# Four conditional layers on one core: products of the weights made first and kept in tables, against two dense layers for every tile of tokens

## The chip, the cores and the metric

The kernel runs on one core of a Trainium2 chip. The core has TensorE (matrix products), VectorE, ScalarE and GpSimd (elementwise work), and SyncE, called SP, which here only issues transfers. They run their own instruction streams and meet at semaphores. The metric is the device time of one execution in microseconds; lower is better.

## The reference

x holds 64 batches of 64 tokens of 1024 numbers. Four layers are added to it, one after the other:

```
x = x + x @ W0.T + 2 * sum over experts e of gate[e] * (x @ A0[e].T) @ B0[e].T
x = x + (Wc[cond[batch]].T mixing the 64 tokens of a batch)
x = x + (x @ B2[id2[batch]].T) @ A2[id2[batch]].T
x = x + x @ W3.T + b3 + 2 * (x @ A3[id3[batch]]) @ B3[id3[batch]]
```

The gates of the first layer are a softmax over the two largest of eight logits, x @ Wr.T plus 5 for the language of the batch. Ranks are 16; there are 8 experts, 16 mixing matrices of 64x64, 64 adapters in the third layer and 32 in the fourth. The four layers are linear but for the gates. All is fp32.

## The kernel before

A tile is 128 tokens, two batches, and there are 32. Every fp32 operand of a dense product is split into a rounded part (hi, type fp32r) and the rest (lo), and a product takes three passes: hi by hi, lo by hi, hi by lo. ScalarE makes the hi part by a rounding copy (`round_to`, L380) and VectorE the lo part by a subtraction (`rest`, L497).

At the start the chunks of W0, B0 and W3, 17 of 512 KB, go through four staging buffers: GpSimd adds the identity for the residual (L348), ScalarE rounds, VectorE or GpSimd subtracts. Both dense weights then stay on the chip.

The tiles run in a software pipeline: step i does the front of tile i (layers 1 to 3) and the back of tile i - 1 (layer 4). Python writes the first two and the last two steps out; those between are a hardware loop (`steps`). TensorE's order in a step is: dense pieces of layer 1 (`layer0`, L711; three pieces of 392, 384 and 384 columns, where the first also holds the expert ranks and the logits), the up product of layer 3 of the tile before (`layer2_up`, L769), the transpose of the gated ranks (L838), the expert rows (`layer0_up`, L752), the dense pieces of layer 4 (`layer3`, L734; up to 384, 352 and 352 columns), mixing in fp32 (L872), the transpose of the stacked ranks (L882), the down product of layer 3 (L892), and the up rows of layer 4 (`layer3_up`, L776). The sum of layer 4 is read from PSUM with the bias added (L696) into outb, and stored.

SP's program holds every transfer of a tile, in an order written out by hand. Where a batch chooses a matrix, SP loads its index from ids_sb into a register first (L232) and then issues a transfer from the chosen row (L241):

```python
return sp.value_load(ids_at[0:1, which, t, b:b + 1], min_val=0, max_val=n - 1)
...
chosen = [index(which, t, b, table.shape[0]) for b in range(BT)]
...
for b in range(BT):
    sp.dma_start(into(b), table[chosen[b]]).then_inc(arrived, 16)
```

ScalarE and VectorE too run through a fixed order in each step: what waits there holds up what is behind it.

Of the kernel before, what the change touches and what calls it, by code (L numbers as in the profile page):

```python
# [5 lines left out]
P = 128  # L6
TOKENS = 128
HALF = 512


def at(i, n):

    return isinstance(i, int) and i == n


class Piece:
# [3 lines left out]
    def __init__(self, shared, start, end):  # L20
        self.x = slice(start, end)
        lead = shared if start == 0 else 0
        self.own = slice(lead, lead + end - start)
        self.bank = slice(0, lead + end - start)
        self.w = slice(0 if start == 0 else shared + start, shared + end)


def cut(shared, edges):
    return [Piece(shared, a, b) for a, b in zip(edges, edges[1:])]


def build(nc, x, W0, A0, Wr, B0, Wc, A2, B2, W3, bias3, A3, B3, lang_ids, ids, out):
# [4 lines left out]
    TILES = x.shape[0]  # L37
    KB = W0.shape[1]
    D = W0.shape[2]
    RANK = B2.shape[3]  # L40
    EXPERTS = Wr.shape[2]
    ER = EXPERTS * RANK
    BT = TOKENS // Wc.shape[1]
    TB = Wc.shape[1]
    BR = BT * RANK
    BANDS = P // BR
    HL = ER + EXPERTS
    HALVES = D // HALF
    D3W = 2 * BR

    PIECES0 = cut(HL, (0, 256, 640, D))
    PIECES3 = cut(D3W, (0, 320, 672, D))
    KH = KB // HALVES
    LANG_BIAS, SCALE0, SCALE3 = 5.0, 2.0, 2.0
    STAGES = 4
    CH_W0, CH_B0, CH_W3, CHUNKS = 0, KB, KB + 1, 2 * KB + 1
    COND, AD2, AD3 = range(3)

    ctx = ExitStack()
    with ctx:  # L60
# [5 lines left out]


        X3_HI, X3_LO, UP3, OUTB = range(CHUNKS - STAGES, CHUNKS)
        stage = [None] * STAGES
        with ExitStack() as stage_ctx:  # L70
            for n in (X3_HI, X3_LO, UP3, OUTB):
                stage[n % STAGES] = stage_ctx.enter_context(nc.sbuf_tensor(f"stage{n % STAGES}", [P, D], F32))
        x3 = pair("x3", [P, KB, TOKENS])
        up3 = sb("up3", [P, D], F32R)
        outb = sb("outb", [P, D])

        w0 = pair("w0", [P, KB, HL + D])
        b0 = pair("b0", [P, D])
        w3 = [sb("w3_hi", [P, KB, D3W + D], F32R),
              sb("w3_lo", [P, KB, D], F32R)]  # L80
        d3 = w3[0][:, :, 0:D3W].rearrange("p k (c b r) -> p k c b r", c=2, b=BT)
        bias_row = sb("bias_row", [P, D])
        xraw = sb("xraw", [P, KB, TOKENS])
        xT = pair("xT", [P, KB, TOKENS])
        with nc.sbuf_tensor("x1", [P, D], F32) as x1:
            pass
        x2 = pair("x2", [P, D])
        upraw = sb("upraw", [P, D])
        up2raw, up3raw = upraw[0:BR, :], upraw[BR:2 * BR, :]
        up2 = sb("up2", [P, D], F32R)  # L90
        d2raw = sb("d2raw", [P, BT, KB, RANK])
        d3raw = sb("d3raw", [P, BT, KB, RANK])
        d2 = sb("d2", [P, KB, 2, BT, RANK], F32R)
        mixraw = sb("mixraw", [P, P])
        mix = sb("mix", [P, P])
        wrraw = sb("wrraw", [P, KB, EXPERTS])
        ident = sb("ident", [P, P])
# [3 lines left out]
        own_batch = sb("own_batch", [BR, BT, TB])  # L101
        iota_e = sb("iota_e", [P, EXPERTS])
        rbias = sb("rbias", [P, TILES, EXPERTS])
        hpart = sb("hpart", [P, BR])
        hsum = sb("hsum", [P, BT, RANK])
        hstack = sb("hstack", [P, BANDS, BT, RANK], F32R)
        h2 = sb("h2", [BR, TOKENS])
# [19 lines left out]

        ps_x1 = [bank(f"ps_x1_{n}") for n in range(len(PIECES0))]
        ps_x23 = [bank(f"ps_x23_{h}") for h in range(HALVES)]
        ps_out = [bank(f"ps_out_{n}") for n in range(len(PIECES3))]  # L130
        ps_d3 = ps_out[0]
        ps_h3T, ps_hgT = ps_x1[2], ps_out[1]
        hi, lo = 0, 1

        def ps_hl(t):

            return ps_x23[1] if at(t, 0) else ps_x1[0]

        def ps_h2(t):

            return ps_out[2] if at(t, 0) else ps_x1[1]
# [3 lines left out]

        def sems(name, n=HALVES):
            return [sem(f"{name}{h}") for h in range(n)]


        ld_x, ld_mix, ld_d2, ld_up2, ld_d3, ld_up3 = map(sem, ("ld_x", "ld_mix", "ld_d2", "ld_up2", "ld_d3", "ld_up3"))  # L150
        ld_ids, ld_lang, ld_bias, ld_a0, ld_wr = map(sem, ("ld_ids", "ld_lang", "ld_bias", "ld_a0", "ld_wr"))
        ld_stage = [sem(f"ld_stage{s}") for s in range(STAGES)]
        st_out = sem("st_out")

        pe_hl, pe_xT, pe_hgT, pe_d2, pe_d3, pe_h3T = map(sem, ("pe_hl", "pe_xT", "pe_hgT", "pe_d2", "pe_d3", "pe_h3T"))
        pe_x2, pe_x3 = map(sems, ("pe_x2", "pe_x3"))
        pe_x1, pe_out = sems("pe_x1", len(PIECES0)), sems("pe_out", len(PIECES3))

        act_w, act_w0d, act_x, act_exp, act_d2, act_up2, act_d3, act_up3, act_hgT, act_fold, act_h2T, act_h3T = map(
            sem, ("act_w", "act_w0d", "act_x", "act_exp", "act_d2", "act_up2", "act_d3", "act_up3", "act_hgT", "act_fold", "act_h2T", "act_h3T"))  # L160
        act_x2, act_x3 = map(sems, ("act_x2", "act_x3"))
        act_x1 = sems("act_x1", len(PIECES0))

        dve_w, dve_w0d, dve_x, dve_diff, dve_hg, dve_up2, dve_d3, dve_up3, dve_hgT, dve_d2, dve_own, dve_h2T, dve_h3 = map(
            sem, ("dve_w", "dve_w0d", "dve_x", "dve_diff", "dve_hg", "dve_up2", "dve_d3", "dve_up3", "dve_hgT", "dve_d2", "dve_own", "dve_h2T", "dve_h3"))
        dve_x2, dve_x3 = map(sems, ("dve_x2", "dve_x3"))
        dve_out = sems("dve_out", len(PIECES3))

        pool_const, pool_w, pool_lo, pool_mix = map(sem, ("pool_const", "pool_w", "pool_lo", "pool_mix"))

        dve_lang, dve_fold, dve_hpart, dve_hsum, dve_h3hi = map(sem, ("dve_lang", "dve_fold", "dve_hpart", "dve_hsum", "dve_h3hi"))
        dve_lg, dve_top, dve_topi, dve_topf, dve_gden, dve_grec, dve_gw0, dve_gw1, dve_gsel, dve_gates = map(
            sem, ("dve_lg", "dve_top", "dve_topi", "dve_topf", "dve_gden", "dve_grec", "dve_gw0", "dve_gw1", "dve_gsel", "dve_gates"))


        PLAN = {"x1 0": 2, "up2 0": 2, "h2 0": 1, "gates 1": 1, "hgT 1": 2}
        assert sum(PLAN.values()) == KB


        POOL_LO = (CH_W3, CH_W3 + 2, CH_W3 + 4)  # L180

        def split_done(n):

            own = n in POOL_LO
            return pool_lo if own else dve_w, sum((m in POOL_LO) == own for m in range(n + 1))


        EXP_AFTER = 3

        def planned(stage):  # L190
            first = CH_W3
            for name, n in PLAN.items():
                if name == stage:
                    return range(first, first + n)
                first += n
            return ()

        CONSTS = 8

        def steps(engine, step):  # L200


            for i in (0, 1):
                step(i, True, i > 0, True)
            with engine.Fori(2, TILES - 1) as i:
                step(i, True, True, True)
            step(TILES - 1, True, True, False)
            step(TILES, False, True, False)

        def split_parts(n):  # L210

            if n < CH_B0:
                return w0[lo][:, n, HL:], w0[hi][:, n, HL:]
            if n == CH_B0:
                return b0[lo][:, :], b0[hi][:, :]
            return w3[lo][:, n - CH_W3, :], w3[hi][:, n - CH_W3, D3W:]

        block = ctx.enter_context(nc.Block())


        @block.sync
        def _(sp):
            ids_at = ids_sb[:, :].rearrange("o (w t b) -> o w t b", w=3, b=BT)

            def load_x(t):

                if not at(t, 0):
                    sp.wait_ge(dve_x, t)
                sp.dma_start(xraw[:, :, :], x[t]).then_inc(ld_x, 16)
# [4 lines left out]
            def load_chosen(t, which, table, into, free, arrived):  # L234

                chosen = [index(which, t, b, table.shape[0]) for b in range(BT)]

                if not at(t, 0):
                    sp.wait_ge(free, t)
                for b in range(BT):  # L240
                    sp.dma_start(into(b), table[chosen[b]]).then_inc(arrived, 16)  # L241

            def load_mix(t):
                load_chosen(t, COND, Wc, lambda b: mixraw[b * TB:(b + 1) * TB, b * TB:(b + 1) * TB], pool_mix, ld_mix)

            def load_down(t, which, raw, table, free, arrived):
                load_chosen(t, which, table, lambda b: raw[:, b, :, :], free, arrived)
# [4 lines left out]
            def load_chunk(n):  # L252

                if n >= STAGES:
                    sp.wait_ge(*split_done(n - STAGES))
# [696 lines left out]
```

## Time and profile before

| what | value |
|---|---|
| median of 3 runs | 995.66 us (994.34 to 996.8) |
| the profiled execution | 994.18 us, span 992.2 us |
| TensorE busy | 979.3 us, 99% of the span |
| VectorE, ScalarE, GpSimd busy | 53%, 37%, 4% |
| DMA | 61.58 MB, mean 62 GB/s |
| mean granted TensorE clock | 0.996 |

The span runs from the first to the last instruction that the profiler saw. Busy shares are of the span. Matmuls are pipelined, so that a single one's time overlaps the next one's; what a matmul costs in a stream is the distance between starts.

### The profile page before, as it was taken

How to read it: one execution, taken by the hardware profiler on the slowest of the kernel's cores; microseconds unless marked ns; L12 is line 12 of the kernel's file. 1: busy time of each engine (PE TensorE's matmuls, PEld its weight loads, DVE VectorE, ACT ScalarE, POOL GpSimd, SP SyncE). 2: the span in 40 equal slices, each digit the busy share in tenths (PEclk: the TensorE clock that was granted, in tenths of full speed). 3: DMA queues.
4: the chain of work that ended last, by engine and by line, in shares of the span. 5: the costliest groups of instructions: out<-in, count | busy, mean ns of one | idle time of the engine just before them, and what ended most of it. 6: DMA issues, size and time to landing. Idle time of an engine off the chain costs nothing.

```text
span 992.2 us, 18376 instructions
## 1 busy us (share of the span) xinstructions
PE 979.3 (99%) x6394; PEld 973.6 (98%) x6394; DVE 530.5 (53%) x1236; ACT 370.3 (37%) x660; POOL 38.1 (4%) x63
## 2 busy tenths in 40 slices
PE   8899999999999999999999999999999999999998
PEld 7799999999999999999999999999999999999998
DVE  5875545545455455455465454554564554554544
ACT  4653332433333343323333323433333333243331
POOL 3600000000000000000000000000000000000000
PEclk9999999999999999999999999999999999999999
DMA  7621111111111111111111111111111111111001
GB/s 257 222 86 55 54 51 54 60 60 39 59 44 59 58 44 57 62 44 58 59 44 54 44 59 58 55 48 59 44 58 59 44 54 50 55 58 62 18 33 43
DMA packets 40046, 61.58 MB, mean 62 GB/s; under 512 B 10849, under 2 KB 27362, under 8 KB 40034
## 3 DMA queue, kind: packets, MB, share of 16 engines
q1 hardware_dynamic: 40034, 61.43, 18.6%
q8 instruction: 6, 0.10, 0.0%
q14 instruction: 6, 0.05, 0.0%
HBM read 44.63 MB, written 16.78 MB: 62 GB/s over the span
## 4 chain that ended last, share of the span: by engine, by line
PE 95%; DVE 3%; DMA 1%; ACT 1%; issue 0%; SPq 0%; POOL 0%; DVEq 0%; POOLq 0%
PE ps_x L711 39%; PE ps_out L734 38%; PE ps_x L872 6%; PE ps_x L752 5%; PE ps_x L892 3%; PE ps_x L769 3%; PE ps_out L776 1%; DMA stage<-w 1%; DVE w_lo L497 1%; DVE up L497 0%; ACT w_hi L380 0%; PE ps_x L882 0%; PE ps_out L838 0%; DVE x_lo L497 0%; DVE topf L564 0%
## 5 line engine op out<-in xcount | busy, mean ns | idle before, releaser
L734 PE MATMUL ps_out<-w_hi,x_hi 128*128 128x352 f32 (+1 forms) x768 | 256.0, 333 | 1.1 <-DVE x_lo L497 1.1
L711 PE MATMUL ps_x<-w_hi,xT_hi 128*128 128x392 f32 (+1 forms) x744 | 257.0, 345 | 0.0
L711 PE MATMUL ps_x<-w_lo,xT_hi 128*128 128x392 f32 (+1 forms) x744 | 252.5, 339 | 0.0
L711 PE MATMUL ps_x<-w_hi,xT_lo 128*128 128x392 f32 (+1 forms) x744 | 252.1, 339 | 0.0
L734 PE MATMUL ps_out<-w_hi,x_lo 128*128 128x352 f32 (+1 forms) x768 | 252.1, 328 | 0.0
L734 PE MATMUL ps_out<-w_lo,x_hi 128*128 128x352 f32 (+1 forms) x768 | 245.7, 320 | 0.0
L380 ACT ACTIVATE up<-upraw 32x1024 fp32r<-32x1024 f32 x128 | 135.1, 1055 | 85.2 <-PE ps_out L776 84.4
L497 DVE TENSOR_TENSOR up<-upraw,up 32x1024 fp32r<-32x1024 f32 x128 | 157.9, 1234 | 3.4 <-ACT up L380 0.5
L734 PEld LDWEIGHTS ps_out<-w_hi,x_hi 128*128 128x128 f32 x768 | 144.6, 188 | 1.2 <-issue 1.2
L734 PEld LDWEIGHTS ps_out<-w_hi,x_lo 128*128 128x128 f32 x768 | 144.6, 188 | 0.0
L734 PEld LDWEIGHTS ps_out<-w_lo,x_hi 128*128 128x128 f32 x768 | 144.5, 188 | 0.0
L711 PEld LDWEIGHTS ps_x<-w_hi,xT_hi 128*128 128x128 f32 x744 | 140.3, 189 | 1.1
L711 PEld LDWEIGHTS ps_x<-w_hi,xT_lo 128*128 128x128 f32 x744 | 140.4, 189 | 0.0
L711 PEld LDWEIGHTS ps_x<-w_lo,xT_hi 128*128 128x128 f32 x744 | 140.3, 189 | 0.0
L497 DVE TENSOR_TENSOR xT_lo<-xraw,xT_hi 128x1024 fp32r<-128x1024 f32 x32 | 39.4, 1232 | 115.0 <-ACT xT_hi L380 115.0
L497 DVE TENSOR_TENSOR x_lo<-ps_x,x_hi 128x512 fp32r<-128x512 f32 x128 | 85.0, 686 | 19.5 <-ACT x_hi L380 19.4
L380 ACT ACTIVATE x_hi<-ps_x 128x512 fp32r<-128x512 f32 x128 | 72.9, 597 | 58.1 <-PE ps_x L872 53.0
L696 DVE TENSOR_TENSOR outb<-ps_out,bias_row 128x352 f32<-128x352 f32 (+1 forms) x96 | 46.2, 510 | 43.4 <-PE ps_out L776 40.7
L553 DVE TENSOR_TENSOR lg<-ps_x,rbias 128x8 f32<-128x8 f32 x32 | 5.3, 167 | 115.9 <-PE ps_x L711 115.8
L380 ACT ACTIVATE x<-ps_x 128x384 f32<-128x384 f32 (+1 forms) x96 | 43.5, 456 | 62.5 <-PE ps_x L752 56.9
L420 ACT ACTIVATE gexp<-gdiff 128x1 f32<-128x1 f32 x32 | 6.5, 202 | 160.2 <-DVE gdiff L559 160.2
L872 PE MATMUL ps_x<-mix,x 128*128 128x128 f32 x512 | 62.4, 275 | 1.0 <-POOL mix L361 1.0
(95 smaller groups left out, 890.5 us busy)
## 6 DMA issues: line engine op xcount, KB each, us to landing
xraw<-x SPq DMA_DIRECT2D x32, 512.0 KB, 3.2
out<-outb SPq DMA_DIRECT2D x31, 512.0 KB, 2.6
stage<-w SPq DMA_DIRECT2D x16, 512.0 KB, 4.9
d2raw<-b SPq DMA_DIRECT2D x64, 64.0 KB, 1.8
upraw<-a SPq DMA_DIRECT2D x64, 64.0 KB, 2.1
d3raw<-a SPq DMA_DIRECT2D x64, 64.0 KB, 1.8
upraw<-b SPq DMA_DIRECT2D x64, 64.0 KB, 2.1
mixraw<-wc SPq DMA_DIRECT2D x64, 16.0 KB, 1.9
```

The costliest lines, as they stand in the source:

```text
L380: return nc.scalar.activation(dst, src, ACT.Copy)
L420: nc.scalar.activation(gexp[:, :], gdiff[:, :], ACT.Exp).then_inc(act_exp, 1)
L497: return nc.vector.tensor_tensor(out=dst, in0=src, in1=rounded.bitcast(F32), op=ALU.subtract)
L553: nc.vector.tensor_tensor(out=lg[:, :], in0=ps_hl(t)[:, ER:HL], in1=rbias[:, t, :], op=ALU.add).then_inc(dve_lg, 1)
L696: nc.vector.tensor_tensor(out=outb[:, piece.x], in0=ps_out[n][:, piece.own], in1=bias_row[:, piece.x], op=ALU.add).then_inc(dve_out[n], 1)
L711: last = nc.tensor.matmul(ps_x1[n][:, piece.bank], xT[a][:, k, :], w0[c][:, k, piece.w], start=k == 0 and m == 0, stop=k == KB - 1 and m = ...
L734: last = nc.tensor.matmul(ps_out[n][:, bank], x3[a][:, k, :], w3[c][:, k, w], start=k == 0 and m == 0, stop=k == KB - 1 and m == len(PASSE ...
L752: up = nc.tensor.matmul(ps_x1[n][:, PIECES0[n].own], hgT[a][:, :], b0[c][:, PIECES0[n].x], start=False, stop=done_last, skip_group_check=True)
L769: last = nc.tensor.matmul(ps_x23[h][:, k * TOKENS:(k + 1) * TOKENS], up2[:, (h * KH + k) * P:(h * KH + k + 1) * P], h2T[:, :], start=False ...
L776: nc.tensor.matmul(ps_out[n][:, piece.own], h3T[:, :], up3[:, piece.x], start=False, stop=True, skip_group_check=True).then_inc(pe_out[n], 1)
L872: last = nc.tensor.matmul(ps_x23[h][:, k * TOKENS:(k + 1) * TOKENS], x1[:, own], mix[:, :], start=k == 0, stop=False, skip_group_check=True)
L892: last = nc.tensor.matmul(ps_h2(f)[0:2 * BR, 0:TOKENS], d2[:, k, :, :, :].rearrange("p c b r -> p (c b r)"), x2[a][:, k * TOKENS:(k + 1) * ...
```

## The change

The kernel becomes two stages. The first makes, in 61 groups of 24 matmuls (8 blocks of 128 by three passes) with 128 stationary and 512 moving columns, the products of weights that the tokens would otherwise meet one after the other: (1 + W0) and B0 with the down matrices of layers 3 and 4 for every adapter (tables t2, t3, stored to device memory), the up matrices of layer 3 with (1 + W3) (table tu2), and (1 + W0) and B0 with (1 + W3), kept on the chip in w and b03. The up matrices of layer 4 are split and stored as tu3. A table holds hi and lo parts, split once.

In the second stage tokens meet one dense product, x by w, whose 1224 columns are the 128 expert ranks, 8 logits, 64 columns of the chosen down tables and 1024 of the product. The experts' rows are added (`experts`), ScalarE and VectorE split the result into y, and the mixing matrix is applied to y in three passes (`mixed`). Rank passes add the chosen up rows of layers 3 and 4 (up2, up3), and a small product of raw matrices (ps_ud) gives what layer 3's rank adds to layer 4's. Step i does the front of tile i and all from ps_ud on of tile i - 1. All tile steps are written out; there is no hardware loop (`tiles` is a Python loop).

The program of TensorE in a step. In the places left out after the waits stand: after ld_up2 the rows of up2 and the product with udb, after dve_hg the transpose of hg, after experts(0) the transpose of h3stack, at the end the rows of up3.

```diff
+            def step(i, par, front, back):
+                if front:
+                    pe.wait_ge(dve_x, f + 1)
+                    pe.wait_ge(pool_md, f + 1)
...
+                    dense(0, par, range(KB)).then_inc(pe_hl, 1)
+                if back:
+                    pe.wait_ge(dve_ud, 2 * b + 2)
...
+                    for k in range(KB):
+                        last = nc.tensor.matmul(ps_ud, u2s[:, k, ...], d3m[:, k, ...], start=k == 0, stop=k == KB - 1)
+                    last.then_inc(pe_ud, 1)
+                    pe.wait_ge(dve_mix, b + 1)
+                    for n in range(3):
...
+                        last = mixed(n)
...
+                    last.then_inc(pe_mix, 1)
+                    pe.wait_ge(dve_va, 2 * b + 2)
+                    nc.tensor.matmul(ps_rep, repeat[...], va[:, :], start=True, stop=True).then_inc(pe_rep, 1)
+                if front:
...
+                    dense(1, par, range(KB))
+                if back:
+                    pe.wait_ge(dve_h2, BT * b + BT)
+                    nc.tensor.transpose(ps_h2T, h2stack[...], ident[:, :]).then_inc(pe_h2T, 1)
+                if front:
...
+                    dense(2, par, range(KB // 2))
+                if back:
+                    pe.wait_ge(act_h2T, b + 1)
+                    pe.wait_ge(ld_up2, 16 * BT * (b + 1))
...
+                if front:
+                    pe.wait_ge(dve_hg, f + 1)
...
+                    dense(2, par, range(KB // 2, KB)).then_inc(pe_y, 1)
+                    pe.wait_ge(dve_hgT, f + 1)
+                    pe.wait_ge(pool_mb, f + 1)
+                    experts(0)
+                if back:
...
+                if front:
+                    experts(1)
+                    experts(2)
+                if back:
+                    pe.wait_ge(act_h3T, b + 1)
+                    pe.wait_ge(ld_up3, 16 * BT * (b + 1))
...
```

That of SP:

```diff
+            def step(i, par, front, back):
+                f, b = i, i - 1
+                if front and not at(i, TILES - 1) and not at(i, 0):
+                    load_x(f + 1, 1 - par)
+                if back:
+                    load_up(b, AD2, NE2, tu2, up2, pe_up2, ld_up2)
+                    load_up(b, AD3, NE3, tu3, up3, pe_out[2], ld_up3)
+                if front and not at(i, TILES - 1):
+                    load_md(f + 1)
+                if front:
+                    load_mix(f)
+                    load_ud(f)
+                if back:
+                    for n in range(3):
+                        sp.wait_ge(dve_out[n], b + 1)
+                    sp.dma_start(out[b], outb[:, :]).then_inc(st_out, 16)
```

`load_md` and `load_ud` load four indices and issue four transfers each, two adapters of either kind: rows of 128 x 2304 bytes from t2 and t3, and raw matrices of 64 KB. `load_up` and `load_mix` load two indices and issue two transfers; a pair of up rows is written to the chip twice over, 256 KB a transfer. Every index is loaded where it is used.

ScalarE's step and VectorE's. In the places left out VectorE makes va, the stacks of h2 and udb; then, behind gate(f), the lo parts of u2s, d3m and mix; the stacks of h3; the lo parts of hgT and of the three y pieces; and last the three sums of ps_o and bias_row into outb.

```diff
+            def step(i, par, front, back):
+                f, b = i, i - 1
+                if front and not at(i, TILES - 1):
+                    x_hi(f + 1, 1 - par)
+                if front:
+                    act.wait_ge(dve_diff, f + 1)
+                    nc.scalar.activation(gexp[:, :], gdiff[:, :], ACT.Exp).then_inc(act_exp, 1)
+                    act.wait_ge(ld_ud, 16 * 2 * BT * (f + 1))
...
+                    for dst, raw in ((u2s, u2raw), (d3m, d3raw)):
+                        round_to(dst[...], raw[:, :, :, :]).then_inc(act_ud, 1)
+                    act.wait_ge(pool_mix, f + 1)
...
+                    round_to(mix[hi][:, :], mixid[:, :]).then_inc(act_mix, 1)
+                if back:
+                    act.wait_ge(pe_h2T, b + 1)
+                    round_to(h2T[:, :], ps_h2T).then_inc(act_h2T, 1)
+                if front:
+                    act.wait_ge(pe_hgT, f + 1)
+                    round_to(hgT[hi][:, :], ps_hgT).then_inc(act_hgT, 1)
+                for n in range(3):
+                    if front:
+                        act.wait_ge(pe_x1[n], f + 1)
+                        round_to(y[hi][:, YS[n]], ps_y[n][:, YK[n]]).then_inc(act_y[n], 1)
+                    if back and n == 0:
+                        act.wait_ge(pe_h3T, b + 1)
+                        round_to(h3T[:, :], ps_h3T).then_inc(act_h3T, 1)
```

```diff
+                if front and not at(i, TILES - 1):
+                    x_lo(f + 1, 1 - par)
+                if back:
+                    dve.wait_ge(pe_ud, b + 1)
+                    nc.vector.tensor_copy(va[:, :], ps_ud[:, 0:BR]).then_inc(dve_va, 1)
...
+                if front:
+                    gate(f)
...
+                if back:
...
+                if front:
...
+                if back:
...
```

In the first stage SP loads a stationary block of 512 KB for every group, three groups ahead; eight pieces of 256 KB of the next moving chunk beside each of the first four chunks; and stores tables: eight stores of 0.59 MB for each of the first three chunks, and two of 256 KB for each block of up rows. GpSimd's new work in a tile is to place the chosen columns into w and b03 (`place_w`, `place_b`) and to add the identity to the mixing matrix.

## Rows read from the trace of the kernel before

**Rows 1.** The page, part 4: the chain that ended last, by line.
```profile
PE ps_x L711 39%; PE ps_out L734 38%; PE ps_x L872 6%; PE ps_x L752 5%; PE ps_x L892 3%; PE ps_x L769 3%; PE ps_out L776 1%; DMA stage<-w 1%; DVE w_lo L497 1%; DVE up L497 0%; ACT w_hi L380 0%; PE ps_x L882 0%; PE ps_out L838 0%; DVE x_lo L497 0%; DVE topf L564 0%
```

**Rows 2.** Windows, one steady tile: length, engines' busy us, granted clock, DMA share, GB/s.
```profile
500.00:530.50 30.50, 30.50 (x202) 30.44 (x201) 16.04 (x40) 11.26 (x21) 0.46 (x1) 1.00 0.16 53
```

**Rows 3.** The chain in order of time, one tile: start us, us, what.
```profile
503.17 2.10 PE ps_x L711 x12
...
510.68 1.78 PE ps_x L872 x16
512.46 3.85 PE ps_out L734 x24
516.31 0.11 PE ps_x L882
516.42 0.96 PE ps_x L892 x16
...
521.78 4.29 PE ps_x L711 x24
```

**Rows 4.** Timeline of SP's queue, a step written out: start us, us, what.
```profile
45.08 1.18 SPq L241 DMA_DIRECT2D mixraw<-wc  x2
47.57 0.89 SPq L241 DMA_DIRECT2D d2raw<-b  x2
48.50 0.43 SPq L229 DMA_DIRECT2D xraw<-x  x1
50.22 0.85 SPq L241 DMA_DIRECT2D upraw<-a  x2
52.38 0.89 SPq L241 DMA_DIRECT2D d3raw<-a  x2
```

**Rows 5.** One line's instructions, L232, same stretch: duration ns min/median/max.
```profile
L232 SPq TENSOR_LOAD <-ids_sb x8: 261/266/267, 46.3 to 53.9; - x8
```

**Rows 6.** Timeline where a tile ends.
```profile
521.82 0.53 DVE L696 TENSOR_TENSOR outb<-ps_out,bias_row 128x352 f32<-128x352 f32 x1 [1.23 <-PE ps_out L776]
...
522.58 0.36 SPq L309 DMA_DIRECT2D out<-outb  x1
```

**Rows 7.** The page, part 6: transfers, KB each, median us from issue to landing.
```profile
xraw<-x SPq DMA_DIRECT2D x32, 512.0 KB, 3.2
...
d2raw<-b SPq DMA_DIRECT2D x64, 64.0 KB, 1.8
```

**Rows 8.** Groups by line: busy us, mean ns of one, then idle before and releaser.
```profile
L497 DVE TENSOR_TENSOR x_lo<-ps_x,x_hi 128x512 fp32r<-128x512 f32 x128 | 85.0, 686 | 19.5 <-ACT x_hi L380 19.4
...
L696 DVE TENSOR_TENSOR outb<-ps_out,bias_row 128x352 f32<-128x352 f32 (+1 forms) x96 | 46.2, 510 | 43.4 <-PE ps_out L776 40.7
...
L497 DVE TENSOR_TENSOR xT_lo<-xraw,xT_hi 128x1024 fp32r<-128x1024 f32 x32 | 39.4, 1232 | 115.0 <-ACT xT_hi L380 115.0
...
L380 ACT ACTIVATE xT_hi<-xraw 128x1024 fp32r<-128x1024 f32 x32 | 33.7, 1053 | 2.3 <-DMA xraw<-x 2.0 <-PE ps_x L800 0.3
...
L380 ACT ACTIVATE d<-d2raw 128x256 fp32r<-128x256 f32 x32 | 13.1, 409 | 0.0
...
L380 ACT ACTIVATE hgT_hi<-ps_out 128x128 fp32r<-128x128 f32 x32 | 8.9, 277 | 86.1 <-PE ps_out L838 86.1
...
L354 POOL TENSOR_TENSOR w_lo<-stage,w_hi 128x1024 fp32r<-128x1024 f32 x3 | 7.6, 2545 | 4.8 <-ACT w_hi L380 4.8
```

**Rows 9.** TensorE's timeline, a pause in brackets, with its releaser.
```profile
44.25 1.11 PE L769 MATMUL ps_x<-h2T,up 128*128 128x128 f32 x8 [2.42 <-DVE h2T L497]
```

**Rows 10.** Windows of 2 us in the first tiles (columns as in rows 2).
```profile
28.00:30.00 2.00, 1.31 (x7) 0.74 (x5) 2.00 (x3) 1.74 (x5) 1.78 (x2) 1.00 1.03 340
...
46.00:48.00 2.00, 2.00 (x8) 2.00 (x8) 1.84 (x5) 0.85 (x2) 1.95 (x3) 0.50 0.38 137
48.00:50.00 2.00, 1.54 (x8) 1.03 (x7) 1.92 (x5) 0.63 (x3) 0.46 (x1) 0.68 0.46 100
```

More of the change, by code:

```diff
@@ L11, in at, with build @@
 def at(i, n):
[L13 to L32, printed above, removed]
+    return i == n
+def build(nc, x, stat, mov, a0, wr, wc, u3, u2k, d3k, bias3, lang_ids, ids, out):
     F32, F32R, I32, U32 = mybir.dt.float32, mybir.dt.float32r, mybir.dt.int32, mybir.dt.uint32
@@ L90, in build, with split_pair @@
[L90 to L93, printed above, removed]
+        def split_pair(name, shape):
+            with nc.sbuf_tensor(f"{name}_raw", shape, F32) as raw:
+                pass
+            lower = sb(f"{name}_lo", shape, F32R)
+            return raw, [sb(f"{name}_hi", shape, F32R), lower]
+        with nc.sbuf_tensor("md_a", [P, PER, 2 * ROW], F32R) as md_a:
+            pass
@@ L176, in build @@
[L176 to L216, printed above, removed]
+        ld_stat = [sem(f"ld_stat{n}") for n in range(RING)]
@@ new lines, in build, with tiles @@
+        pe_x1 = [sem(f"pe_x1{n}") for n in range(3)]
+        pe_out = [sem(f"pe_out{n}") for n in range(3)]
+        CONSTS = 6
+        SETS = BT + 6
+        def tiles(engine, step):
+            step(0, 0, True, False)
+            step(1, 1, True, True)
+            for j in range(1, TILES // 2 - 1):
+                step(2 * j, 0, True, True)
+                step(2 * j + 1, 1, True, True)
+            step(TILES - 2, 0, True, True)
+            step(TILES - 1, 1, True, True)
+            step(TILES, 0, False, True)
@@ L231, in index, with load_x, load_md @@
+            def load_x(t, par):
+                if not at(t, 0) and not at(t, 1):
+                    sp.wait_ge(pe_y, t - 1)
+                sp.dma_start(xraw[par][:, :, :], x[t]).then_inc(ld_x[par], 16)
             def index(which, t, b, n):
                 return sp.value_load(ids_at[0:1, which, t, b:b + 1], min_val=0, max_val=n - 1)
[L234 to L236 removed]
+            def load_md(t):
+                chosen = [(t2, index(AD2, t, b, NE2)) for b in range(BT)] + [(t3, index(AD3, t, b, NE3)) for b in range(BT)]
@@ new lines, in load_up @@
+            def load_up(t, which, n, table, up, used, arrived):
+                chosen = [index(which, t, b, n) for b in range(BT)]
+                if not at(t, 0):
+                    sp.wait_ge(used, t)
+                for b in range(BT):
+                    twice = table[chosen[b]].rearrange("h r c -> (h r) c")[None].to_broadcast([2, 2 * RANK, D])
+                    sp.dma_start(up[b * 2 * BR:(b + 1) * 2 * BR, :].bitcast(F32), twice.bitcast(F32)).then_inc(arrived, 16)
+            sp.wait_ge(pool_const, CONSTS)
@@ L322, in _ @@
+            tiles(sp, step)
+            sp.wait_ge(st_out, 16 * TILES)
         @block.gpsimd
@@ L356, in mix_identity, with place_b @@
+            def place_b(t):
+                if not at(t, 0):
+                    pool.wait_ge(pe_x1[0], t)
+                for part in (hi, lo):
+                    rows = mdraw[:, :, part * ROW + KB * RANK:(part + 1) * ROW]
+                    last = nc.gpsimd.tensor_copy(b03[part][:, 0:MD].rearrange("p (q r) -> p q r", r=RANK), rows)
+                last.then_inc(pool_mb, 1)
             def mix_identity(t):
@@ L450, in step @@
-                    if at(i, 0):
-                        x_hi(1)
-                    split(f"hgT {i}")
-                    down_hi(f, ld_d2, pe_d2, d2, d2raw, act_d2)
-                    for n, piece in enumerate(PIECES0):
-                        act.wait_ge(pe_x1[n], f + 1)
-                        round_to(x1[:, piece.x], ps_x1[n][:, piece.own]).then_inc(act_x1[n], 1)
-                if more and not at(i, 0):
-                    x_hi(i + 1)
-                split(f"x1 {i}")
-                if back and front:
-                    up_hi(f, ld_up2, pe_x3[1], up2, up2raw, act_up2)
@@ L660, in step @@
                 if front:
                     dve.wait_ge(act_hgT, f + 1)
-                    rest(hgT[lo][:, :], ps_hgT[:, 0:TOKENS], hgT[hi][:, :]).then_inc(dve_hgT, 1)
-                    if at(i, 0):
-                        chunk_lo(CH_B0)
-                        x_lo(1)
-                    split(f"hgT {i}")
-                    down_lo(f, act_d2, d2, d2raw, dve_d2)
-                if more and not at(i, 0):
-                    x_lo(i + 1)
-                if back:
-                    h3_stack(b)
@@ L672, in step @@
-                split(f"x1 {i}")
-                if back and (at(i, 1) or not front):
-                    up3_lo()
-                if front:
-                    for h in range(HALVES):
-                        dve.wait_ge(act_x2[h], f + 1)
-                        own = slice(h * HALF, (h + 1) * HALF)
-                        rest(x2[lo][:, own], ps_x23[h][:, :], x2[hi][:, own]).then_inc(dve_x2[h], 1)
-                    up_lo(f, act_up2, up2, up2raw, 0, dve_up2)
-                    down_lo(f, act_d3, d3, d3raw, dve_d3)
-                    split(f"up2 {i}")
-                    h2_sum(f)
-                    h2_lo(f)
-                    split(f"h2 {i}")
+                    rest(hgT[lo][:, :], ps_hgT, hgT[hi][:, :]).then_inc(dve_hgT, 1)
@@ new lines, in dense, with experts @@
+            def dense(n, par, ks):
+                for k in ks:
+                    for m, (a, c) in enumerate(PASSES):
+                        last = nc.tensor.matmul(ps_y[n][:, 0:YB], xT[par][a][:, k, :], w[c][:, k, Y[n]],
+                                                start=k == 0 and m == 0, stop=k == KB - 1 and m == len(PASSES) - 1)
+                return last
+            def experts(n):
+                for m, (a, c) in enumerate(PASSES):
+                    last = nc.tensor.matmul(ps_y[n][:, YK[n]], hgT[a][:, :], b03[c][:, YS[n]],
+                                            start=False, stop=m == len(PASSES) - 1, skip_group_check=True)
+                last.then_inc(pe_x1[n], 1)
@@ L909 @@
+                    for n in range(3):
+                        nc.tensor.matmul(ps_o[n][:, OK[n]], h3T[:, :], up3[:, OX[n]], start=False, stop=True,
+                                         skip_group_check=True).then_inc(pe_out[n], 1)
+            tiles(pe, step)
 def kernel(x, itok_B_0_7, itok_B_0_15, itok_B_4_50, itok_B_0_23, L0_cond_W, L0_cond_Wr, L0_cond_A, L0_cond_B,
```

1033 lines of the change are left out of this document (521 added, 512 removed).

## The prediction, made before the changed kernel ran

> **What bounds the kernel now.** I read the chain that ended last first: see in it that two dense products, L711 and L734, hold 39% and 38% of the span [rows 1]. The window of one steady tile shows TensorE busy for all of its 30.50 us, VectorE for 16, ScalarE for 11, and the DMA engines at 16% [rows 2]. The stores of successive tiles are 30.2 us apart. So 32 tiles of 30.2 us are 966 us, and filling and draining take the other 26. A change pays if it takes matmul time out of a tile and leaves every other engine and queue inside the time that is left.
>
> **What a matmul costs.** The chain by pieces, in order of time, gives the spacing [rows 3]: 24 matmuls of 392 columns take 4.29 us (179 ns each), 12 of 384 columns 2.10 (175), 24 of 352 columns 3.85 (160). That is columns at 2.4 GHz plus 13 to 15 ns. I carry the line on: 408 columns 185 ns, 512 columns 228 ns. If the extra grew with the width as it does from 352 to 392, they would be 187 and 237, and if it stayed at 13, 183 and 226. Narrow ones: 16 of 128 columns with 64 stationary 0.96 us (60 ns each), a transpose 0.11, eight fp32 products of 128 columns 1.78 (0.22 each).
>
> TensorE: Matmul & The Clock Gate, in the Trainium skill, section Back-to-back issue gap, gives a sustained 131 ns for a 512-column matmul in a stream with weight loads. No row here is at 512, but 352 columns already take 160 ns, so the trace disagrees. By the page the first stage below would be 192 us in place of 334, and the forecast 1088.
>
> **New first stage.** 61 groups of 24 matmuls of 512 columns: 61 x 24 x 0.228 = 334 us. Beside each group of 5.47 us VectorE does a 1024-wide subtraction (1.23), a 512-wide one from PSUM (0.69) and at most two more of 512, some 3.3 us in all; ScalarE does less [rows 8]. Both are covered. The transfers are tighter. In the third chunk one group goes with 0.52 MB of stationary block, 0.26 of moving piece, 0.26 of up rows, 0.52 of stored rows and 0.59 of stored table: 2.16 MB in 5.47 us, 395 GB/s, while the loading window with full DMA engines moved 340 [rows 10]. At 340 a group would take 6.35 us: 0.9 more over 8 groups, and less in the fourth chunk (1.9 MB). The stationary blocks are loaded three groups ahead, which absorbs 10 us of that. I take 3 us, ends 0 and 15. The first group needs 2.6 MB: 7.7 us at 340 GB/s behind a first landing near 4 us, then its splitting: it ends at about 14 us. Stage end: 14 + 60 x 5.47 + 3 = 345 us.
>
> **TensorE's work in a tile afterwards.** Dense 72 x 0.185 = 13.3; mixing 3 at 384 and 6 at 352 columns, 1.48; expert rows 3 at 272 (0.125 by the line) and 6 at 408, 1.49; the 64-column product of eight, 0.5; the repeat 0.25; three transposes 0.33; second-layer rows 0.53, third-layer rows 0.47. Sum 18.35 us against 30.2. Were this all, 32 tiles would take 587 us and the kernel about 945.
>
> **The other engines in a tile.** VectorE loses four band subtractions of 32x1024 and gains the small stacks: below 12 us. GpSimd places 2 x 512 columns: its widest row, 1024 columns, takes 2.55 us [rows 8], so about 3 us, and up to 12 us would still fit between the rows' landing and the next tile. Both are covered.
>
> **SP's queue, the step that decides.** After the change SP issues in every tile, in this order: the store of the tile before, x for the next tile, two rows of up-table 2, two of up-table 3, four of the down tables, two mixing matrices, four raw adapter matrices (load_ud). Ahead of them stand 14 loads of an index into a register. The old unrolled tiles show the prices with nothing to wait for [rows 4]: a pair of issues 0.85 to 0.89 us (mixing 1.18), and between the end of one pair and the start of the next, where two index loads stand, 47.57 - 46.26 = 1.31 us (again 1.29 and 1.31). The load itself is 0.27 us [rows 5]; register arithmetic makes up the rest. Hence one index costs 0.65 us, one issue 0.43. From the store's issue to the start of the last load_ud issue:
> store 0.41 + x 0.43 + up2 (1.31 + 0.86) + up3 (1.31 + 0.86) + down 4 x (0.65 + 0.44) + mixing (1.31 + 1.18) + load_ud 4 x 0.65 + 3 x 0.44 = 15.9 us.
> The order makes this a wait. The store must follow the last eviction of its tile. Let T0 be the moment at which TensorE starts a tile. The last y piece leaves PSUM late: ScalarE rounds it until T0 + 0.2, VectorE subtracts until 0.8, then three evictions of 0.51 [rows 8] end at 2.4, and SP's store follows 0.23 later, as now (522.35 to 522.58) [rows 6]: T0 + 2.6. The last load_ud issue starts at T0 + 18.5 and lands 1.8 us later [rows 7]: T0 + 20.3.
> ScalarE's program has the rounding of u2raw and d3raw of the front tile, then that of mix, ahead of h2T of the back tile. It waits for load_ud, then takes 0.41 + 0.41 + 0.28 + 0.28 [rows 8]: h2T is there at T0 + 21.7. Queued behind it on ScalarE are hgT, h3T and the y pieces. TensorE needs h2T after dense 0 (4.44), the product of eight (0.5), mixing (1.48), repeat (0.25), dense 1 (4.44), a transpose (0.11) and half of dense 2 (2.22): at T0 + 13.4. It waits 8.3 us in sum. What follows is 0.53 + 0.11 + 2.22 + 0.38 + 0.11 + 1.11 + 0.47 = 4.9 us: the tile takes 26.6 us.
>
> **The other wait, hidden inside it.** x lands at T0 + 3.0 + 3.2 [rows 7] + 0.9 behind the store. ScalarE (1.05) and VectorE (1.23) [rows 8] split it before VectorE reaches va, two operations of some 0.2: T0 + 9.9. TensorE wants va for the repeat at T0 + 6.4. This wait of 3.5 us comes before the h2T wait and is taken out of its 8.3, leaving 4.8.
>
> **The clock.** TensorE's pause of 2.42 us before 44.25 [rows 9] was followed by a granted clock of 0.50 and 0.68 in two windows of 2 us, one of the chip's two levels, 1.2 GHz, for part of them: 1.0 + 0.64 = 1.6 us of work lost [rows 10]. Both pauses here are longer. A loss behind the first is hidden by the second wait. One behind the second lies on the path as far as it falls within the 4.9 us: I take 1.3 (ends 0 and 4.9, all of it at 1.2 GHz). Tile: 27.9 us.
>
> **The sum.** Stage 345. Tile 0 has no back part, but its load_ud comes after the bias, down and mixing issues: its mix and hgT wait until 15.8, end 17.3. Tile 1's queue starts early, so it takes 19.8. Tiles 2 to 30: 29 x 27.9 = 809. Tile 31 lacks x and the down tables in the queue: 22.8. The last back part is a chain of store, up rows, two stacks, evictions and the store: 14. Span 345 + 17.3 + 19.8 + 809 + 22.8 + 14 = 1228, and 2 us outside the span as in the profiled execution now (994.18 against 992.2; its median of three runs, 995.66, is 1.5 higher): **1230 us**. The 421 us that are not tiles 2 to 30 put the point of no change at (994 - 421) / 29 = 19.8 us a tile.
>
> **Rivals.**
> 1. The forecast: SP's queue sets the tile. Chance 0.70.
> 2. The queue keeps up (index loads overlapping when four stand together, issues cheaper without register arithmetic), and x's chain binds: tile 9.9 + 18.35 - 6.4 = 21.9, time 413 + 29 x 21.9 = 1048. For it: the index load is only 0.27 us of the 0.65. Against: the 1.3 us gaps come from unrolled tiles like the new ones. 0.10.
> 3. TensorE stays the bound, tile 18.35, 945 us, faster. It needs load_ud on the chip by T0 + 11.8 and x about 3.5 us earlier, that is a queue of under 8 us where the rows give 15.9; it decides from 19.8 us a tile. For it: TensorE has been the bound throughout. 0.05.
> 4. The clock falls for all that follows the wait: tile 26.6 + 4.9 = 31.5, time 1335. For it: two pauses in each tile, longer than the one in the rows. Against: the old dip was short. 0.12.
> 5. Wide matmuls leave the line and stay at the 175 ns of 384 columns: 61 x 24 x 0.053 = 78 us less, 1152. Against: the three widths in rows 3 rise with the columns. 0.02. (The page's figure above would be a stronger form of this.)
> A chance of 0.01 is left to no change.
>
> **Range.** Tiles of 25.7 (no clock loss, an index at 0.6) to 30.2 us, stage ends included: 421 + 745 = 1166 to 421 + 876 = 1297. So 1165 to 1300. Chances: faster by over 0.3% 0.05, within 0.3% (what a measurement of this kernel can tell from no change, given runs of 994.34 to 996.8) 0.01, slower 0.94.
>
> **What the new profile would show.** Right: TensorE busy without pauses until about 345 us, then repeated gaps, its share of busy time near 75%; stores of tiles some 28 us apart; before h2T ScalarE waiting for DMA u2raw or d3raw; a second TensorE wait at the repeat, on VectorE's va; 15 issues filling SP's queue; granted clock below 1 in the second stage only. Wrong: stores under 22 us apart (the index price), matmuls of 512 columns far from 228 ns (the line), or gaps in the first stage (transfers). If SP's chain runs ahead by any way that I misread, the prediction fails by over 180 us.

## The result

The changed kernel takes 1665.88 us (median of 4 runs, 1660.94 to 1667.49) against 995.36 us, 1.673 times as long, 95% interval 1.668 to 1.677. The prediction was 1230 us, 1165 to 1300: right in the direction and in the place of the loss, too low by 436 us, outside its range.

The page of the changed kernel, parts 1, 2 and 4, where [rows 1] had two dense products with 39% and 38%:

```profile
PE 1055.9 (63%) x5018; PEld 961.8 (58%) x5018; DVE 473.8 (28%) x1362; ACT 257.4 (15%) x524; POOL 89.0 (5%) x218
...
PEclk9999999998777777777777777777777777777776
...
SPq 41%; PE 27%; DMA 16%; issue 9%; DVE 4%; ACT 3%; POOL 0%; DVEq 0%; ACTq 0%
SPq L349 15%; SPq L356 14%; PE ps_o L780 10%; DMA d3raw<-d3k 10%; PE ps_y L787 7%; SPq L381 5%; PE ps_v L780 4%; DMA tu<-rows_lo 4%; DVE outb L757 3%; SPq L364 2%; PE ps_y L793 2%; SPq L372 2%; PE ps_o L862 1%; DMA up<-tu 1%; PE ps_o L857 1%
```

TensorE has given way to SP's queue: the index loads (L349), the issues of the down tables (L356) and the landing of the raw matrices hold 39% of the chain. Windows over the two stages (length, TensorE, its weight loads, VectorE, ScalarE, GpSimd, granted clock, DMA share, GB/s):

```profile
0.00:352.00 352.00, 342.37 (x1498) 282.05 (x1499) 149.68 (x178) 123.21 (x172) 27.00 (x62) 1.00 0.64 210
352.00:1660.00 1308.00, 712.30 (x3519) 678.98 (x3517) 322.73 (x1181) 134.17 (x352) 61.98 (x156) 0.76 0.22 72
```

The first stage is dense, as forecast, and the second is not; nearly all the clock loss is in the second (0.97 between 150 and 200 us, else 1.00 in the first). SP's queue over one steady tile, where [rows 4] had pairs of issues at 0.85 to 0.89 us (timeline: start us, us, what):

```profile
937.64 0.35 SPq L410 DMA_DIRECT2D out<-outb  x1
938.04 0.42 SPq L346 DMA_DIRECT2D x_raw<-x  x1
940.49 4.56 SPq L381 DMA_DIRECT2D up<-tu  x4
947.97 8.45 SPq L356 DMA_DIRECT2D mdraw<-t  x4
957.73 1.21 SPq L364 DMA_DIRECT2D mixraw<-wc  x2
961.34 0.34 SPq L372 DMA_DIRECT2D u2raw<-u2k  x1
961.88 0.33 SPq L373 DMA_DIRECT2D d3raw<-d3k  x1
962.39 0.33 SPq L372 DMA_DIRECT2D u2raw<-u2k  x1
962.90 0.33 SPq L373 DMA_DIRECT2D d3raw<-d3k  x1
978.57 0.35 SPq L410 DMA_DIRECT2D out<-outb  x1
```

From store to store it is 40.93 us, where 27.9 was forecast. The four issues of mdraw take 8.45 us, although each is only 144 KB (rows of 1152 bytes; the section on the change gives 2304, which is wrong by a factor of two). ScalarE over the same tile:

```profile
946.68 0.20 ACT L564 ACTIVATE gexp<-gdiff 128x1 f32<-128x1 f32 x1 [3.41 <-DVE gdiff L686]
968.32 0.42 ACT L491 ACTIVATE u2s<-u2raw 128x256 fp32r<-128x256 f32 x1 [21.45 <-DMA d3raw<-d3k]
968.65 0.40 ACT L491 ACTIVATE d3m<-d3raw 128x256 fp32r<-128x256 f32 x1
968.95 0.29 ACT L491 ACTIVATE mix_hi<-mixid 128x128 fp32r<-128x128 f32 x1
969.15 0.26 ACT L491 ACTIVATE h2T<-ps_t 128x128 fp32r<-128x128 f32 x1
```

It stands 21.45 us before the rounding of u2raw, with h2T behind it. That is the forecast's wait. What is new are windows of the same tile in which little should be moving: the last up load had been issued by 945.05, and mdraw's issues began at 947.97.

```profile
944.00:946.00 2.00, 1.11 (x6) 1.07 (x7) 1.80 (x9) 0.00 (x0) 0.00 (x0) 1.00 0.13 37
946.00:948.00 2.00, 2.00 (x8) 1.97 (x7) 1.72 (x12) 0.20 (x1) 0.00 (x0) 0.54 0.13 37
948.00:950.00 2.00, 2.00 (x8) 1.97 (x8) 0.80 (x4) 0.00 (x0) 0.00 (x0) 0.61 0.13 49
...
958.00:960.00 2.00, 0.00 (x0) 0.00 (x0) 0.00 (x0) 0.00 (x0) 0.00 (x0) 0.50 0.19 65
960.00:962.00 2.00, 0.00 (x0) 0.00 (x0) 0.00 (x0) 0.00 (x0) 0.00 (x0) 0.50 0.13 54
```

From 944 to 966 us the DMA share stays at 0.13 and more; it is 0.08 from 966 to 968 and zero behind that. 0.13 is two of 16 engines, here at 37 to 54 GB/s. That became theory A: the repeated load of up rows, whose source has an outermost dimension of 2, runs on two engines only. DMA: Bandwidth & Descriptors, in the Trainium skill, section Why a DMA increments its semaphore by 16 and not by 1, states just that: a transfer is spread over the largest number of engines, at most 16, that divides the slowest dimension larger than 1 on both sides. The trace agrees, with its 0.13.

### The profile page after: what moved, and what is told of

Its sections match the earlier page's. It is cut to its first block, busy times and chain, and to the rows that moved or that the text cites. A ratio compares the mean times of both kernels' runs of the same rounds, so it can differ in the third digit from the quotient of the medians.

```text
span 1665.7 us, 15636 instructions
## 1 busy us (share of the span) xinstructions
PE 1055.9 (63%) x5018; PEld 961.8 (58%) x5018; DVE 473.8 (28%) x1362; ACT 257.4 (15%) x524; POOL 89.0 (5%) x218
## 4 chain that ended last, share of the span: by engine, by line
SPq 41%; PE 27%; DMA 16%; issue 9%; DVE 4%; ACT 3%; POOL 0%; DVEq 0%; ACTq 0%
SPq L349 15%; SPq L356 14%; PE ps_o L780 10%; DMA d3raw<-d3k 10%; PE ps_y L787 7%; SPq L381 5%; PE ps_v L780 4%; DMA tu<-rows_lo 4%; DVE outb L757 3%; SPq L364 2%; PE ps_y L793 2%; SPq L372 2%; PE ps_o L862 1%; DMA up<-tu 1%; PE ps_o L857 1%
## 5 line engine op out<-in xcount | busy, mean ns | idle before, releaser
L787 PE MATMUL ps_y<-w_hi,x_hi 128*128 128x408 f32 x768 | 312.4, 407 | 0.0
L787 PE MATMUL ps_y<-w_hi,x_lo 128*128 128x408 f32 x768 | 300.5, 391 | 0.0
L787 PE MATMUL ps_y<-w_lo,x_hi 128*128 128x408 f32 x768 | 297.6, 387 | 0.0
L787 PEld LDWEIGHTS ps_y<-w_hi,x_hi 128*128 128x128 f32 x768 | 171.4, 223 | 7.0 <-issue 0.3
L787 PEld LDWEIGHTS ps_y<-w_hi,x_lo 128*128 128x128 f32 x768 | 169.8, 221 | 1.6
L787 PEld LDWEIGHTS ps_y<-w_lo,x_hi 128*128 128x128 f32 x768 | 169.0, 220 | 2.0
L780 PE MATMUL ps_o<-chunk_a_hi,stat_hi 128*128 128x512 f32 x216 | 84.5, 391 | 4.4 <-DVE stat_lo L593 4.4
L593 DVE TENSOR_TENSOR stat_lo<-stat_raw,stat_hi 128x1024 fp32r<-128x1024 f32 x61 | 75.4, 1235 | 36.6 <-ACT stat_hi L491 35.6
L780 PE MATMUL ps_o<-chunk_a_hi,stat_lo 128*128 128x512 f32 x216 | 84.1, 389 | 0.0
L780 PE MATMUL ps_o<-chunk_a_lo,stat_hi 128*128 128x512 f32 x216 | 84.1, 389 | 0.0
```

The source lines that it names most:

```text
L593: return nc.vector.tensor_tensor(out=dst, in0=src, in1=rounded.bitcast(F32), op=ALU.subtract)
L780: last = nc.tensor.matmul(ps_g[g % BANKS][:, :], st[g % RING][a][:, k, :], mchunk[c % 2][v][:, k, :], start=k == 0 and m == 0, stop=k == K ...
L787: last = nc.tensor.matmul(ps_y[n][:, 0:YB], xT[par][a][:, k, :], w[c][:, k, Y[n]], start=k == 0 and m == 0, stop=k == KB - 1 and m == len( ...
```

## The experiments

Tile times below are the distance from the first to the last of the 32 stores, over 31. The expectations count the experiments in another order than this text: their first, third, fifth and sixth are experiments 1, 5, 7 and 8 here.

**1. Up rows by all engines.** Besides these lines TensorE's two waits for the up rows count twice as many arrivals.

```diff
-                    twice = table[chosen[b]].rearrange("h r c -> (h r) c")[None].to_broadcast([2, 2 * RANK, D])
-                    sp.dma_start(up[b * 2 * BR:(b + 1) * 2 * BR, :].bitcast(F32), twice.bitcast(F32)).then_inc(arrived, 16)
+                    once = table[chosen[b]].rearrange("h r c -> (h r) c")
+                    for c in (0, 1):
+                        rows = slice((2 * b + c) * BR, (2 * b + c + 1) * BR)
+                        sp.dma_start(up[rows, :].bitcast(F32), once.bitcast(F32)).then_inc(arrived, 16)
```

> Edit: each pair of up rows is loaded by two transfers with 32 rows as the outermost dimension, in place of one transfer that repeats the 32 rows with an outermost dimension of 2. Nothing else changes. Theory A (the repeated load runs on only two of the 16 DMA engines, so that 1 MB a tile piles up there, blocks the queue in front of the table loads and delays load_ud): the four issues of mdraw fall from 8.4 us to about 2 us, u2raw and d3raw land in about 2 us instead of 5.4, four more issues cost about 2 us; tile 40.9 us to about 32.5, time near 1400 us. Theory B (the table loads themselves are dear: 1152-byte rows from tables in device memory): mdraw's issues stay above 1 us each, tile stays near 40 us, time above 1600 us.

Measured: 1339.17 us, ratio 1.346 (1.342 to 1.350); tile 30.3 us against 40.6 in the changed kernel. SP's timeline in a tile:

```profile
768.06 4.83 SPq L383 DMA_DIRECT2D up<-tu  x8
775.29 1.93 SPq L356 DMA_DIRECT2D mdraw<-t  x4
```

mdraw's issues fell from 8.45 to 1.93 us and the raw matrices land in 1.8 us (median), as before the change [rows 7]. Theory B, dear table loads, is out: same rows, same tables. The first window after the up rows is at share 0.07, not 0.13:

```profile
774.00:776.00 2.00, 2.00 (x12) 2.00 (x12) 1.72 (x12) 0.20 (x1) 0.00 (x0) 1.00 0.07 16
```

The edit also turned four transfers of 256 KB into eight of 128 KB; the next experiment takes that apart from the shape.

**2. The control: bytes and count of experiment 1, outermost dimension 2.** It leaves the lo rows of the up tables out: hi rows stand in their place, 16 rows read twice in place of 32 read once.

```diff
-                    once = table[chosen[b]].rearrange("h r c -> (h r) c")
+                    once = table[chosen[b]][0:1].to_broadcast([2, RANK, D])
```

> The first experiment with one thing taken back: each of its eight 128 KB loads of up rows now reads 16 rows twice, with an outermost dimension of 2 (the lo rows are left out of the computation, hi rows stand in their place). Bytes, count of transfers and order are those of the first experiment. Theory A, by the outermost dimension: 1 MB a tile again piles up on two engines, mdraw's issues are again near 2 us each and load_ud lands late: tile 41 to 43 us, time near 1690 us. If the size of a transfer or the number of them made the difference, the time stays at 1339 us.

Measured: 1612.22 us, ratio 1.620 (1.617 to 1.623); tile 38.8 us. So 273 us lie between this and experiment 1, with bytes, count and order the same: they come from the shape of the access. (That 16 rows are read twice here is not the cause: experiments 8 and 9 read the same 32 rows.) It was 5% under the forecast. SP's issues differ from those of the changed kernel:

```profile
760.46 7.99 SPq L383 DMA_DIRECT2D up<-tu  x8
771.42 2.46 SPq L356 DMA_DIRECT2D mdraw<-t  x4
```

One of mdraw mostly took 0.34 us, as in experiment 1, though the same bytes went to the two engines. One of up rows took 0.63 in place of 0.34, and never under 0.61, the very first of them included, ahead of which no other up load stood: this part is a price of the shape, not of a backlog. Why mdraw's issues are dear in the changed kernel and not here, no run shows; they begin 11.0 us after the first up issue here and 7.5 there, so less may be waiting.

**3. Order of SP's queue.** load_ud and load_mix stand directly behind load_x, up rows and down tables after them; up rows as in the changed kernel.

```diff
                     load_x(f + 1, 1 - par)
+                if front:
+                    load_ud(f)
+                    load_mix(f)
                 if back:
...
                     load_md(f + 1)
-                if front:
-                    load_mix(f)
-                    load_ud(f)
```

> Edit: SP loads the raw matrices and the mixing matrices of the front tile directly behind x, ahead of the up rows and the down tables; up rows are still loaded by one repeating transfer each. Theory A: the wait for h2T goes, but the up rows' 1 MB on two engines lands some 20 us after its first issue, and TensorE then waits for up3 or the down tables: tile about 33 us, time near 1440 us. Theory B: up rows land soon, only the down tables are late; tile 28 to 30 us, time near 1300 us. Should the order of the queue not matter, the time stays at 1666 us.

Measured: 1541.68 us, ratio 1.550 (1.545 to 1.554); tile 36.7 us, 3.7 more than theory A gave. The chain in order of time shows what took the place of h2T's wait:

```profile
781.16 0.61 SPq L381
781.98 0.55 SPq L381
782.57 0.78 SPq L349
784.36 0.58 SPq L381
785.14 20.84 DMA up<-tu
806.11 0.40 PE ps_o L883
```

The last of four up loads, 1.05 MB together, lands 20.8 us after its issue and 24.8 after the first one's: 42 GB/s for these rows over the whole of it, beside the two engines' part of the other transfers. At full share all 16 engines moved 340 in the kernel before [rows 10] and up to 426 in slices of the changed one, so an estimate for two is 43 to 53. The loop is store, 13.7 us of queue, 20.8 us of landing, the matmuls of up3, evictions, store; the expectation had counted 20 us from the first up issue.

**4. The reordering elsewhere: ScalarE's and VectorE's programs.** SP is untouched.

```diff
-                    act.wait_ge(ld_ud, 16 * 2 * BT * (f + 1))
...
-                    round_to(mix[hi][:, :], mixid[:, :]).then_inc(act_mix, 1)
                 if back:
                     act.wait_ge(pe_h2T, b + 1)
...
                         round_to(h3T[:, :], ps_h3T).then_inc(act_h3T, 1)
+                if front:
+                    act.wait_ge(ld_ud, 16 * 2 * BT * (f + 1))
...
+                    round_to(mix[hi][:, :], mixid[:, :]).then_inc(act_mix, 1)
```

and the lo parts of u2s, d3m and mix go behind VectorE's evictions in the same way.

> The changed kernel with one reordering: ScalarE rounds u2raw, d3raw and mix at the end of a tile's step, behind y, and VectorE subtracts their lo parts behind the evictions, so that h2T and hgT no longer stand behind load_ud. SP's program is untouched. If the forecast's place of the wait is right, TensorE no longer waits for h2T; with 1 MB on two engines the next thing late is up3 or the down tables, some 33 us into the tile, and the tile falls from 40.9 to about 34 us, time near 1480 us. If h2T's wait was not what set the tile, the time stays within 1% of 1666 us.

Measured: 1326.88 us, ratio 1.335 (1.331 to 1.338); tile 29.9 us; the expectation had the direction, and a time 12% too high. Three instructions each, moved later on two engines that are 15% and 28% busy, are worth 339 us. That is the forecast's wait for h2T, shown at its place. The rest is the up rows again: the chain reads store, 6.9 us of queue, landing, evictions.

```profile
790.22 0.59 SPq L381
791.02 21.39 DMA up<-tu
```

Experiment 3 has 6.8 us more of queue ahead of the landing, and a tile that is 6.8 us longer.

**5. Experiments 1 and 3 together.**

> Both edits together. Theory A: SP's own issuing (14 index loads of 0.65 us, 19 issues) is left, about 20.5 us from the store to the last table load; the down tables, last in the queue, land at about 25 us into the tile and the next tile starts after place_w: tile about 26.5 us, time near 1220 us. Theory B: tile above 30 us, because the table loads are dear wherever they stand.

Measured: 1089.11 us, ratio 1.095 (1.092 to 1.098); tile 22.5 us, where 26.5 was expected. I had let a tile start 25 us after the last start, but SP's chain begins at the store, and while TensorE waits for the down tables the evictions and the store are already done. In other tiles x is late instead (5.1 us of landing behind the store at 751.62); x holds 8% of the chain.

**6. The index loads.** Experiment 1, with fixed rows in place of chosen ones.

```diff
-                return sp.value_load(ids_at[0:1, which, t, b:b + 1], min_val=0, max_val=n - 1)
+                return (5 * t + 3 * b + which) % n
```

> The first experiment without the 14 index loads of a tile: every batch takes fixed rows of the tables, so the choice by index is left out of the computation; transfers, sizes and order stay. If an index load costs SP 0.65 us on the path, the tile falls by 9.1 us from the first experiment's, to about 23.5 us, or to 21.9 us where x's chain takes over; time near 1130 us. If index loads overlap with the transfers and cost nothing, the tile stays as in the first experiment.

Measured: 1131.21 us, ratio 1.137 (1.118 to 1.156); tile 23.6 us, 6.7 under experiment 1. Now x's chain bounds the tile, rival 2 of the forecast, with each of its pieces in the chain:

```profile
774.95 0.34 SPq L412
775.29 0.04 issue
775.34 4.75 DMA x_raw<-x
780.11 1.06 ACT x_hi L493
781.20 1.23 DVE x_lo L595
782.42 0.10 DVE va L721
782.55 0.19 DVE va L723
782.74 0.04 issue
782.78 0.40 PE ps_v L839 x2
```

x lands 4.75 us after its issue, where the forecast had 3.2 + 0.9. The two runs, 1123.28 and 1139.13 us, lie further apart than those of the others, so the gain of 208 us over experiment 1 is known to some 10 us.

**7. x earlier.** Experiment 5, with load_x(f + 2, par) ahead of SP's wait for the evictions, and none at the head of the step.

> The third experiment, and x for the tile after next is loaded before SP waits for the evictions of the tile, not behind its store. If x's chain (store, x, ScalarE, VectorE, va) still stops TensorE at the repeat, its wait of some 3 to 4 us a tile goes and SP's own 20.0 us of issuing is the tile: about 20.8 us, time near 1045 us. If SP's issuing alone was the bound before, nothing changes from 1089 us.

Measured: 1081.7 us, ratio 1.086 (1.084 to 1.088); tile 22.2 us. The time is near the expectation's second case, by another way: x no longer stops TensorE, and almost nothing is gained, because the tile starts when the down tables, last in the queue but for x, have landed and GpSimd has placed them. Most stores are 20 to 21 and 23 to 25 us apart by turns. The chain shows it as a pause between two tiles:

```profile
724.34 0.47 PE ps_o L885 x3
724.81 3.13 issue
727.93 6.23 PE ps_y L789 x24
```

**8. Fewer index loads.** Experiment 7, with the registers of a tile's adapter indices kept: load_md loads them, load_ud and load_up take them again; 6 loads a tile in place of 14.

```diff
+            kept = {}
...
+                if which == COND:
+                    return sp.value_load(ids_at[0:1, which, t, b:b + 1], min_val=0, max_val=n - 1)
+                if (which, t, b) not in kept:
+                    kept[which, t, b] = sp.value_load(ids_at[0:1, which, t, b:b + 1], min_val=0, max_val=n - 1)
+                return kept[which, t, b]
```

> The fifth experiment, and the indices of the adapters of a tile are loaded once and their registers kept for the raw matrices and the up rows: 6 index loads a tile in place of 14. At 0.65 us each SP's chain falls from 20.0 to about 14.8 us, below TensorE's 18.35 us of work, and the tile is TensorE's: 18.4 to 19 us, time 950 to 970 us, faster than the kernel before. If something other than SP binds (waits on VectorE, the clock), the tile stays above 20 us.

Measured: 984.72 us (median of 5), ratio 0.990 (0.987 to 0.994): faster than the kernel before by 1% (its slowest run 989.93, the fastest of the kernel before 994.37), and 681 us faster than the change as it was given. It lies 15 us above the expected band: 7 from the first stage, the rest from tiles of 19.3 us where 18.4 to 19 were expected (the mean of the first 29; the last are shorter). Tile 19.0 us over all, and TensorE is the bound again (windows over the same two stages):

```profile
0.00:352.00 352.00, 340.31 (x1500) 279.74 (x1501) 148.61 (x178) 123.30 (x173) 29.07 (x62) 1.00 0.63 210
352.00:960.00 608.00, 598.51 (x3459) 580.66 (x3458) 312.60 (x1158) 134.79 (x345) 62.45 (x156) 1.00 0.52 153
```

**9. Experiment 8 with the up rows on two engines again.**

> The sixth experiment with the repeating loads of up rows as in the changed kernel, 256 KB each with an outermost dimension of 2. If those run on two engines at some 52 GB/s together, 1.05 MB takes 20 us and those engines' sixteenth of the other 2.3 MB about 5 us more: tile about 26 us, time near 1200 us, slower than the kernel before. If the queue's index loads and order were all that mattered, the time stays near 985 us.

Measured: 1430.14 us, ratio 1.438 (1.431 to 1.446); tile 33.2 us. One access shape costs 445 us in a kernel that is otherwise TensorE's. The expectation of 26 us was a rate over the tile. The transfer is in a loop: its last issue waits for the store of the tile before, then 23.0 us of landing follow, of which nothing overlaps the next one's:

```profile
776.42 22.96 DMA up<-tu
```

## Why the prediction was off, step by step

- **First stage, right.** 345 us were forecast; TensorE takes up the tiles at 352.3. Its matmuls of 512 columns are 5.44 us for 24, 227 ns (forecast 228; of the two other ways to carry the line on, the wide one is 234 by its own rows, not 237). The second group waited for its stationary block until 15.8, and the full DMA engines around 150 to 200 us cost 5.5 us of TensorE's time, where the sum had 3 for all transfers.
- **TensorE's work in a tile, right.** 18.35 us forecast; 18.9 from start to start in experiment 8. Rival 3 fails for the kernel as changed, but its state is reached once the queue lets it; rival 5 fails on the 227 ns.
- **SP's queue decides, and h2T behind load_ud is where TensorE stops: right.** Experiments 3 to 6 and 8 show it from both sides: moving the wait brought 339 us in experiment 4, leaving the index loads out 208 between experiments 1 and 6. The wait for va at the repeat, hidden inside it, is there too: 2.8 us before 944.89, forecast 3.5. The price of 0.65 us an index was near: four of them stand in 2.4 us in experiment 1, 0.60 each, and 2.9 in the changed kernel.
- **The step that failed is the term "up2 (1.31 + 0.86) + up3 (1.31 + 0.86) + down 4 x (0.65 + 0.44)", with the landing of 1.8 us after it.** It took the new transfers at the price of old ones of 64 KB, and SP's own time as all that decides when the raw matrices land. Measured from 938.46 to 956.42, that part took 18.0 us in place of 8.7, and d3raw landed after 5.4 in place of 1.8: 12.9 us. With 29 such tiles that is 374 of the 436 us. The cause is the shape of the up loads (experiments 1 and 2, 8 and 9): on two engines they take some 25 us a tile, counted from the first issue (24.8 in experiment 3, 25.2 in 9), and the raw matrices, issued behind them, land at about the time when that is through. From the first up issue they took 27.8 us in the changed kernel, about 25.8 in the control, where mdraw's issues were cheap, and 25.5 in the changed kernel's last tile, where no down tables stand between and the time is in the landing instead:

```profile
1598.64 0.63 SPq L381
...
1613.85 10.30 DMA d3raw<-d3k
```

  So how the loss splits between SP's issues and the landing says little: the sum of both stays near the time of the transfer on two engines. I had added up its bytes, 1.05 MB a tile, and not asked how many engines would carry them. That the raw matrices wait because parts of them stand behind the up rows on those two engines fits this, but no view here shows a single engine.
- **The clock, near.** From h2T to the next store 9.15 us went by, where 4.9 + 2.6 with 1.3 for the clock makes 8.8. Granted was 0.50 from 958 us to beyond 970. The pieces of the sum are 26.6 + 12.9 + 1.3 = 40.8; measured 40.9. Rival 4, the whole rest of the tile at the lower clock, did not happen.
- **The ends, too low.** Tiles 0, 1 and 31 and the last back part were put at 74 us and took about 126: the same queue. The last up load alone held the end for 20.0 us in the chain, from 1640.40 on.
- **The range** was built on the price of an index and on the clock. Its lower tile, no clock loss and an index at 0.6, adds up to 25.9 us, not 25.7, which changes nothing here. No end of it held a doubt of what a kind of transfer that the old trace did not have would cost, though one row there could not speak for it.

## What to carry to other kernels

When an engine loses work, draw the loop that closes a tile: what is issued only after this tile's last write, and which engine's program puts something urgent behind its landing. A queue of 14 register loads and 16 issues is a bound of its own (18.5 us from the store to the last raw matrix in experiment 1, where each issue is cheap), and moving one wait behind work that is due earlier, or loading an index once, can be worth more than the matmuls saved. And count the engines of a new transfer by the outermost dimensions of both sides before its bytes are added up.

## What the hardware showed that I had not expected

- A load whose source repeats 32 rows with an outermost dimension of 2 held 2 of 16 DMA engines (share 0.13), and four of them, 1.05 MB, landed 20 to 23 us after the last issue, some 25 after the first; the same bytes as eight loads with 32 outermost rows landed in a median of 2.6 us each.
- Behind such loads SP's issue of mdraw took a median of 1.38 us (up to 3.47) in place of 0.34, and mdraw landed after 5.5 us in place of 2.2. In the control, with the same bytes on two engines, the issue was back at 0.34 and the landing at 2.8; the reason stays open.
- The issue of a load of 128 KB took SP 0.63 us with an outermost dimension of 2 and 0.34 with 32.
- Halving the transfers of this kind to 128 KB, still two engines each, brought 54 us (1666 to 1612); the dimension brought 273 more.
